# Six more weight units by in-place Prelu chains, other engines for three norms and four factors, and earlier joins in one window

## What is computed

```python
xn = layernorm(x)
K  = s4_kernel(...)                       # 512 taps from a 64-state model
conv = irfft(rfft(xn, 2L) * rfft(K, 2L))[:L] + D * xn
Wg, Wu, Wd = NF4_CODE[q] * absmax per block of 64   # 1792x512, 1792x512, 512x1792
h  = silu(xn @ Wg.T) * (xn @ Wu.T)
out = x + conv + h @ Wd.T
```

## Time and profile before

| | us |
|---|---|
| median of 3 runs | 469.33 (469.02 to 470.54) |
| the profiled execution, its own time | 468.54 |
| its span in the profile | 466.8 |
| PE busy | 436.9 (94%) |
| DVE busy | 400.3 (86%) |
| ACT busy | 279.8 (60%) |
| POOL busy | 205.0 (44%) |

### The profile page before, as it was taken

How to read it: one execution, slowest core, us unless ns; L and a number is a source line. 1 busy time by engine, 2 the same in 40 slices (tenths; PEclk the granted TensorE clock), 3 DMA queues, 4 the chain that set the end, 5 groups by cost and what they waited for, 6 DMA issues and landing times.

```text
span 466.8 us, 7247 instructions
## 1 busy us (share of the span) xinstructions
PE 436.9 (94%) x2544; PEld 248.0 (53%) x2544; DVE 400.3 (86%) x627; ACT 279.8 (60%) x475; POOL 205.0 (44%) x188
## 2 busy tenths in 40 slices
PE   0589999998994999999999999999999999999997
PEld 0444444443441444444444444466544688888886
DVE  5889958989987789898897778969898899999993
ACT  7956647477778686686775767946132543545340
POOL 0493586464958586456665555948400000000000
PEclk9999999999998999999999999999999999999999
DMA  8381636021514363151522142347693021101111
GB/s 283 79 289 69 136 76 157 24 68 46 181 34 148 116 197 137 46 181 46 180 68 68 37 115 78 92 162 241 197 345 136 1 91 46 38 10 46 46 47 45
DMA packets 34168, 51.41 MB, mean 110 GB/s; under 512 B 13076, under 2 KB 14164, under 8 KB 33364
## 3 DMA queue, kind: packets, MB, share of 16 engines
q1 hardware_dynamic: 34132, 50.95, 35.2%
HBM read 38.03 MB, written 10.81 MB: 105 GB/s over the span
## 4 chain that ended last, share of the span: by engine, by line
PE 64%; DVE 12%; POOL 11%; issue 5%; DMA 5%; ACT 3%; SPq 1%; POOLq 0%; DVEq 0%; ACTq 0%
PE bank L2278 27%; PE bank L2405 21%; PE bank L2355 8%; PE bank L2345 6%; DMA lines<-wd 3%; POOL work L879 2%; PE bank L2125 2%; DVE h L1421 1%; POOL w L892 1%; POOL h L784 1%; DMA work<-in_q_up 1%; DVE work L1351 1%; DVE h L1437 1%; DVE work L1347 1%; DVE h L1475 1%
## 5 line engine op out<-in xcount | busy, mean ns | idle before, releaser
L966 ACT ACTIVATE work<-work 128x512 f32<-128x512 f32 (+1 forms) x210 | 115.3, 622 | 13.1 <-POOL work L879 8.1
L879 POOL TENSOR_SCALAR work<-work 128x512 f32<-128x512 int32 x35 | 75.3, 2152 | 58.6 <-DVE work L1347 54.1
L2278 PE MATMUL bank<-h 128*128 128x512 f16 x360 | 81.7, 379 | 0.8 <-DVE h L1411 0.6
L2125 PE MATMUL bank<-xT,w 128*128 128x512 f16 (+1 forms) x300 | 64.5, 371 | 3.3 <-DVE w L1361 1.8
L2278 PEld LDWEIGHTS bank<-h 128*128 128x128 f16 x360 | 35.1, 98 | 44.3 <-issue 2.3
L2405 PE MATMUL bank<-wd,work 128*128 128x256 f16 x504 | 56.2, 273 | 0.0
L2278 PE MATMUL bank<-xT,w 128*128 128x512 f16 x240 | 55.4, 379 | 0.0
L2405 PEld LDWEIGHTS bank<-wd,work 128*128 128x128 f16 (+1 forms) x504 | 49.3, 98 | 6.0
L892 POOL TENSOR_SCALAR w<-work,sc 128x512 f16<-128x512 f32 x21 | 39.7, 1889 | 23.7 <-DVE work L1351 23.1
L2125 PEld LDWEIGHTS bank<-xT,w 128*128 128x128 f16 x300 | 29.1, 98 | 36.1 <-DVE w L1361 2.1
L1287 ACT ACTIVATE work<-h 128x896 f16<-128x896 f32 x30 | 27.9, 943 | 28.4 <-DVE h L2033 18.3
(11 more groups left out here) (198 smaller groups left out, 687.2 us busy)
## 6 DMA issues: line engine op xcount, KB each, us to landing
moved<-h SPq DMA_DIRECT2D x6, 1024.0 KB, 5.1
h<-moved SPq DMA_DIRECT2D x4, 1536.0 KB, 15.3
h<-in_x SPq DMA_DIRECT2D x8, 512.0 KB, 5.4
xT<-in_x SPq DMA_DIRECT2D x16, 256.0 KB, 3.7
out<-xT SPq DMA_DIRECT2D x15, 256.0 KB, 2.0
work<-in_q_gate SPq DMA_DIRECT2D x14, 256.0 KB, 2.9
work<-in_q_up SPq DMA_DIRECT2D x14, 256.0 KB, 3.4
work<-in_am_gate SPq DMA_DIRECT2D x28, 128.0 KB, 3.0
```

Source lines behind the costliest of these rows:

```text
L879: pool.tensor_scalar(chain_room(u, "r"), qs[:, u % 2, :], RIGHT_FROM, RIGHT_FROM, ALU.max, ALU.subtract).then_inc(first_done, 1)
L966: nc.scalar.activation(room, qs[:, u % 2, :] if j == 0 else room, KNEE, scale=scale, bias=bias, alpha=below).then_inc(knee_done, 1)
L2125: mm = nc.tensor.matmul(out_b, weights(k)[:, unit, wl, f, :], xT[:, TPC * c + first:TPC * c + last, xl, f, :], start=(i == 0), stop=(i == ...
L2278: mm = nc.tensor.matmul(out_b, weight(wl, f), token(xl, f), start=(n == 0 and i in (1, 5)), stop=(n == 5), skip_group_check=i not in (1, 5))
```

## The change

Five things.

1. Units 1 to 6 become chained too (`CHAINED` starts at 1). Their first pass is made by POOL, their six passes by ACT in the order l0, l1, l2, r0, r1, r2 (`SIDES_ORDER`), their high halves still by ACT. RIGHT and LEFT on DVE and `clamp` on ACT go away for them. The rooms of the sides and of the whole change with it, and with them what is waited for.
2. Norms of tiles 1 to 3 go from ACT to POOL; statistics of tile 4 go from ACT to DVE; the factors of chunk 1 go from POOL (17 operations) to DVE (12 operations).
3. The lists of the opening are written anew around this. On PE the 128 x 6 matmul that spreads the weight scales comes before `turn(1)`, and products of tile 1 are dealt between turns 4 to 7.
4. In window 5 the two joins of product 6 stand together right behind the first items; in mixed window 3 join (0, 3, 1) and `h_mul(15)` stand ahead of `token_whole(1, 3)` and an item.
5. On ACT `block_hi(3, 1)` comes before `copy_m1(0, 3)`, and the first two eighths of window 5's passes stand ahead of that window's `block_hi`.

```diff
+SIDES_ORDER = ("l0", "l1", "l2", "r0", "r1", "r2")
+def order_of(u):
+    return SIDES_ORDER if u < 7 else CHAIN_ORDER
-CHAINED = range(7, UNITS)
-POOL_HALVES = CHAINED
+CHAINED = range(1, UNITS)
+POOL_HALVES = range(7, UNITS)
...
         def chain_room(u, side):
-            return knee[:, u % 2 + (2 if side == "r" else 0), :]
+            right = side == "r"
+            if u in (3, 4):
+                return knee_1[:, 2 * (u - 3) + right, :]
+            return knee[:, (0 if u % 2 else 2) + right, :]
         def room_read(u):
-            return dq_after(u - 1, LEFT) if u == CHAINED[0] else dq_after(u - 2, WHOLE)
+            return None if u < 3 else dq_after(0, LEFT) if u < 5 else dq_after(u - 4 if u < 7 else u - 2, WHOLE)
...
-        SUMMED = (1, 4)
+        SUMMED = (1,)
+        POOL_NORMS = 1
...
@@ POOL's list @@
-            rstd(1)
+            first_pass(1)
+            for t in range(POOL_NORMS, TPC):
+                norm(t)
+            first_pass(2)
+            first_pass(3)
             for t in range(TPC, 2 * TPC):
                 norm(t)
+            first_pass(4)
+            first_pass(5)
             for i in range(14):
                 v_step(i)
+            first_pass(6)
...
@@ ACT's list @@
-            knees(1)
-            stats(4)
-            clamp(1)
-            for t in range(TPC):
-                norm(t)
+            chain(1, 0, 5)
+            norm(0)
+            chain(1, 5, 6)
+            chain(2, 0, 1)
...
-            make_knee(4, 2)
-            make_knee(4, 3)
+            chain(4, 0, 3)
             silu(0)
-            make_knee(4, 0)
-            make_knee(4, 1)
-            clamp(4)
-            make_knee(5, 2)
-            make_knee(5, 3)
+            chain(4, 3, 6)
+            chain(5, 0, 3)
             h_hi(0)
-            make_knee(5, 0)
-            make_knee(5, 1)
             silu(1)
             weight_hi(4)
-            clamp(5)
+            chain(5, 3, 6)
             h_hi(1)
...
             silu(12)
+            block_hi(BLOCKED[0], 1)
             copy_m1(0, BLOCKED[0])
-            block_hi(BLOCKED[0], 1)
...
@@ DVE's list, mixed window 3 @@
                     token_whole(1, 2)
+                    join(0, k, 1)
+                    h_mul(n + 3)
                     token_whole(1, 3)
+                    part(4, 6)
...
@@ DVE's list, window 5 @@
                     token_lo(1, 1)
                     stage_of(0, 2)
+                    join(0, k, 0)
+                    join(1, k, 0)
                     token_lo(1, 2)
-                    stage_of(2, 4)
-                    join(0, k, 0)
-                    stage_of(4, 5)
+                    stage_of(2, 5)
                     token_lo(1, 3)
                 stage_of(5, 6)
-                join(1, k, 0)
+                if both:
+                    join(1, k, 0)
...
@@ PE's list @@
             turn(0)
-            turn(1)
             pe.wait_ge(one_done, 1)
             pe.wait_ge(sc_done, 7)
             nc.tensor.matmul(bank[0][:, P:P + 6], ones[:], dg3, start=True, stop=True).then_inc(mx_bc, 1)
+            turn(1)
...
             turn(4)
+            products(1, (0,))
             turn(5)
-            products(1, (0,))
             turn(6)
+            pe.wait_ge(b_cp, 1)
+            pe.wait_ge(wlo_done, PLACE[3] + 1)
+            product(1, 1, 0, 2)
             turn(7)
-            pe.wait_ge(b_cp, 1)
-            products(1, (1,))
+            product(1, 1, 2, TPC).then_inc(up_done, 1)
```

More of the change, by code:

```diff
@@ L237, in ffn_conv_kernel @@
         knee, acc, qs, am, sil = rows_of(0, KNEES), rows_of(4, 3), rows_of(7, 2).bitcast(I32), rows_of(9, 2), rows_of(11, 2)
-        acc_l, acc_r, wt = (acc[:, i, :] for i in range(3))
         ident = sb("ident", [P, P], F32)
@@ L550, in ffn_conv_kernel @@
         OS_AT = {3: 1, 1: 2, 2: 3, 6: 4}
-        FIRST_STEPS = [(0, RIGHT), (0, LEFT), (1, RIGHT), (0, WHOLE), (0, SCALED), (1, LEFT), (1, WHOLE), (2, RIGHT),
-                       (1, SCALED), (2, LEFT), (3, RIGHT), (2, WHOLE), (3, LEFT), (2, SCALED), (3, WHOLE), (3, SCALED)]
         FIRST_BANK = (0, 4)
@@ L945, in make_knee @@
                     act.wait_ge(q_ld[u % 2], 16 * (u // 2 + 1))
-                reader = RIGHT if k >= 2 else LEFT
-                if u >= 2:
-                    act.wait_ge(dq_done, dq_after(u - 2 if u < 9 else u - 1, reader))
                 scale, bias, below = NF4_KNEES[k]
@@ L954, in chain_pass @@
             def chain_pass(u, j):
-                side, i = CHAIN_ORDER[j][0], int(CHAIN_ORDER[j][1])
+                order = order_of(u)
+                side, i = order[j][0], int(order[j][1])
                 room = chain_room(u, side)
                 if i:
-                    act.wait_ge(knee_done, PASSES_AT[u] + CHAIN_ORDER.index(f"{side}{i - 1}") + 1)
+                    act.wait_ge(knee_done, PASSES_AT[u] + order.index(f"{side}{i - 1}") + 1)
                 elif side == "r":
@@ L972, in knees, with chain @@
                     make_knee(u, k)
+            def chain(u, first, last):
+                for j in range(first, last):
+                    chain_pass(u, j)
             def clamp(u):
@@ L1174, in _ @@
             silu(2)
-            knees(6)
+            chain(6, 0, 6)
             silu(3)
-            clamp(6)
             silu(4)
@@ L1183, in _ @@
             x_hi(15)
-            for j in range(len(CHAIN_ORDER)):
-                chain_pass(7, j)
+            chain(7, 0, 6)
             silu(5)
@@ L1228, in mixed_window @@
                 part(k, 6, 8)
+                if k > 3:
+                    part(k + 1, 0, 2)
                 block_hi(k + 1, 0)
@@ L1249, in window @@
                     token_hi(1, 3)
-                    part(k, 0, 3)
+                    part(k, 2, 3)
                 part(k, 3, 6)
@@ L1605, in _ @@
             rstd(0, 5)
-            step(1, RIGHT)
+            step(0, WHOLE)
             rstd(0, 6)
@@ L1618, in _ @@
             scales(5)
+            stats(4)
+            scales(6)
+            step(0, SCALED)
             stats(5)
-            scales(6)
-            step(0, WHOLE)
             stats(6)
-            step(0, SCALED)
             scales(7)
@@ L1627, in _ @@
             moments(4, 8)
+            step(1, WHOLE)
+            rstd(1, 0)
+            rstd(1, 1)
+            rstd(1, 2)
             x_lo(0)
-            step(1, LEFT)
+            rstd(1, 3)
+            weight_lo(0)
+            rstd(1, 4)
             x_lo(1)
-            weight_lo(0)
-            step(1, WHOLE)
+            rstd(1, 5)
+            step(1, SCALED)
+            rstd(1, 6)
+            rstd(1, 7)
             x_lo(2)
-            step(2, RIGHT)
-            step(1, SCALED)
+            rstd(1, 8)
             x_lo(3)
+            rstd(1, 9)
+            rstd(1, 10)
             weight_lo(1)
-            step(2, LEFT)
-            step(3, RIGHT)
+            rstd(1, 11)
+            scales(9)
             step(2, WHOLE)
-            scales(9)
-            step(3, LEFT)
+            scales(10)
             step(2, SCALED)
-            scales(10)
+            scales(11)
+            weight_lo(2)
+            stats(8)
             step(3, WHOLE)
-            weight_lo(2)
+            scales(12)
             step(3, SCALED)
-            stats(8)
             x_lo(4)
-            scales(11)
+            x_lo(5)
             weight_lo(3)
-            x_lo(5)
-            scales(12)
             stats(9)
@@ L1667, in _ @@
             rstd(2, 3)
-            items(23, 24)
+            step(4, WHOLE)
             rstd(2, 4)
             rstd(2, 5)
-            items(24, 25)
+            step(4, SCALED)
             rstd(2, 6)
@@ L1678, in _ @@
             rstd(2, 11)
-            items(25, 26)
-            items(26, 27)
             weight_lo(4)
             h_lo(1)
-            items(28, 29)
+            step(5, WHOLE)
             x_lo(8)
-            items(29, 30)
+            step(5, SCALED)
             stats(12)
@@ L1696, in _ @@
             h_mul(3)
-            items(30, 31)
-            items(31, 32)
-            items(33, 35)
+            step(6, WHOLE)
+            step(6, SCALED)
             h_mul(4)
@@ L1755, in mixed_window @@
                     token_lo(1, 0)
-                part(4, 6)
-                join(0, k, 1)
-                h_mul(n + 3)
+                    part(4, 6)
+                    join(0, k, 1)
+                    h_mul(n + 3)
                 token_sum(1, 0 if k == 3 else 3)
@@ L2152, in turn @@
             def turn(t):
-                if t < TPC:
+                if t < POOL_NORMS:
                     pe.wait_ge(xn_done, t + 1)
                 else:
-                    pe.wait_ge(xp_done, t - TPC + 1)
+                    pe.wait_ge(xp_done, t - POOL_NORMS + 1)
+                if t >= TPC:
                     pe.wait_ge(xlo_done, t - TPC + 1)
```

60 lines of the change are left out of this document (26 added, 34 removed).

## The result

| | before | after |
|---|---|---|
| median of 13 runs each, us | 469.80 | 472.31 |
| lowest to highest | 467.88 to 471.90 | 469.58 to 475.07 |
| the profiled execution, its own time | 468.54 | 471.57 |
| its span | 466.8 | 469.7 |
| PE, DVE, ACT, POOL busy | 436.9, 400.3, 279.8, 205.0 | 440.0, 396.7, 280.8, 209.1 |

The ratio is 1.0051, 95% interval 1.0029 to 1.0074: the changed kernel is slower by about 2.4 us. I had forecast 468.8 us, no change, range 466.2 to 471.6. The sign is wrong and the time lies outside the range.

The account below looks back on a forecast made before the run. PE was taken to bound the kernel, busy 94% of the span, so only its idle gaps could give time. Opening +1.5 and middle -2.0 made -0.5 us on the median 469.33: 468.8 us, no change, range 466.2 to 471.6.

Parts of the forecast that it names:

- The walk of the opening: Engine lists walked with assumed durations up to the gathering of tiles 12 to 15: 53.2 instead of 52.68, +0.5 us.
- whatever moves 52.68 moves PE: DVE's gathering of the last four tiles' statistics at 52.68 moves DVE's stretch from 71.65, and PE waiting there.
- The toll of POOL: Ahead of SCALED of unit 1, POOL's new passes and norms lengthen DVE steps: about +1.0 us, bounds 0 and 2.0.
- The rival in which POOL blocks DVE for whole operations: DVE's steps from 8 to 20 us held for whole POOL operations: 475.3 us, half of it 472; chance 0.12.
- Opening: New opening lists, walk +0.5 plus POOL's toll +1.0: +1.5 us, bounds -0.8 and +3.1.
- (a): block_hi(3, 1) ahead of copy_m1(0, 3): DVE's 0.46 and PE's 0.55 waits go, 0.5 us sooner.
- (d): Four passes pulled ahead of block_hi(5) take some 2.1 us on ACT, which waits there anyway: 0.
- (b): Join (0, 3, 1) earlier: PE's 1.38 at 108.46 goes but is given back before join (0, 4, 0): 0.
- (c): Window 5 joins earlier: product 4 of tile 5 2.7 us sooner, six slow matmuls cost 1.2: -1.5 us.
- the joins give nothing: Rival: DVE late at SCALED before unit 13's high half, product 4 starts as now: 470.8 us, slower; chance 0.12.
- my signs of being right: No join wait before window 5's product 3, 4 to 5 us at product 4, passes 0.66 apart, gathering at 54.2.
- those of being wrong: Gathering of tiles 12 to 15 before 52.7 or after 56, or product 4 within 2 us of its products 7.

Follow-up runs that it names:

- warm run: Changed kernel with 12 extra matmuls of 256 columns between turn(3) and the first product; 471.85 us, ratio 1.0049.
- opening alone: Changed kernel with parts 4 and 5 of the change taken back; 472.36 against 469.66 us, ratio 1.0053.
- joins-only run: Kernel before with only the two joins of window 5 put together; 469.83 against 469.49 us, ratio 0.9993.

## Why the prediction was wrong

**The walk of the opening: +0.5 forecast.** The step that failed is "`h_hi(0)` starts at 39.5": it came at 41.88. The dependent pass was right (three of one side in 1.94, so (1.94 - 0.62)/2 = 0.66 from one to the next). From the split of tile 7 on, my walk held: it had 6.1 us to `h_hi(0)`, and 35.77 to 41.88 is 6.11.

What failed lies ahead of it: I had that split on ACT end near 33.4 and it ended at 35.87, with 4.8 us of standing for turns 5 and 7. Two causes can be told apart. The slow first products, which I did not expect at all: in the warm run, without them, `h_hi(0)` starts at 40.38, 1.5 sooner. And PE's own new list, part 3 of the change: turn 5 now stands behind the 12 matmuls at 27.97, and turn 7 behind the product at 33.33, which waits 1.74 for the low half of unit 3, which waits for ACT, which waits for turn 5. In the warm run, with its fast start, ACT still stands 1.62 and 2.33 for these two turns. No run put the turns back ahead of the products, so what their order costs, and whether that cures the opening as well as unit 4's passes do, stays open. Moving these passes into the waits brought `h_hi(0)` to 40.30 with the same slow products.

**What the opening moves.** I wrote that whatever moves 52.68 moves PE, and watched that row alone. My own walk had unit 5's low half end at 49.7, though PE before had reached that point at about 49 (12 matmuls of 2.75 into the 48 at 46.31) without a wait. So a second path, unit 5 straight to PE, was already late in my own numbers. That half ended at 51.56 + 0.75 = 52.31, and PE's 2.59 sets the end as much as the gathering does: the warm run freed one path and the other took over, for there PE came 1.5 sooner together with unit 5. The run that moved unit 4's passes brought unit 5 sooner and not PE.

**The toll of POOL: +1.0.** Right in kind, and no more than that. DVE, then POOL's norms (22.20) and a first pass (28.50):

```profile
19.00 0.68 DVE L1354 SCALAR_TENSOR_TENSOR work<-work 128x512 f32<-128x512 f32 x1
...
23.63 1.07 DVE L1354 SCALAR_TENSOR_TENSOR work<-work 128x512 f32<-128x512 f32 x1
...
28.65 1.00 DVE L1354 SCALAR_TENSOR_TENSOR work<-work 128x512 f32<-128x512 f32 x1
```

```profile
22.20 3.90 POOL L789 TENSOR_SCALAR h<-h 128x512 f32<-128x512 f32 x4 [3.90 <-DVE h L1584]
...
28.50 1.92 POOL L885 TENSOR_SCALAR work<-work 128x512 f32<-128x512 int32 x1
```

Steps of 0.68 take 1.07 under a norm and 1.00 under a first pass. But I had put the toll ahead of SCALED of unit 1, and that ended at 19.00 + 0.68 = 19.68, where my walk without the toll had 19.7: two small steps there took 0.53 and 0.58 instead of 0.17 (at 15.79 and 16.43, under first passes), and nothing of it shows at the end of SCALED. The rival in which POOL blocks DVE for whole operations, and with it the rule of the Trainium skill (SBUF — State Buffer, Who interferes with whom), would have held the step at 28.65 until the first pass of 28.50 ends at 30.42, 1.8 us; it was longer by 0.3. The measurement decides against the rule for first passes. For norms it doesn't: the norm over the step at 23.63 ends at 24.16, and a step of 0.68 from there would end at 24.84, where this one ends at 24.70. And POOL pays too: the norms at 11.44 and 13.52 take 0.77 each, the one at 12.20, into which DVE's SCALED of 12.38 falls, 1.33, while that DVE step keeps 0.67. So a norm and such a step seem to take turns, with now one and now the other waiting. In the stretch that the rival names, 8 to 20 us, only the two small steps were longer, 0.8 us together; that its half price, 472, is near the measured 472.3 is chance. No experiment took the first passes away from POOL, so the sum of the toll was not measured by itself.

**Opening: forecast +1.5, measured +2.5** (interval of the opening alone 1.6 to 3.4). A mis-sized term, inside its bounds of -0.8 and +3.1, and near the right size in part by luck: the walk, for which I had +0.5, is where the runs find the loss, and the toll of +1.0 doesn't show at its place.

**(a) `block_hi`: -0.5.** PE's 0.55 went and DVE's 0.46 too; not run alone. (d) the passes pulled ahead, forecast 0, were not run alone either.

**(b) Join (0, 3, 1): "given back, 0".** This step failed in its mechanism: it was +1.3, and I had given it no bound. I took join (0, 4, 0) as "isn't moved"; in the run with this edit alone it starts at 123.16, before at 121.74, since DVE itself was late. I asked when PE would need the join and not when `h_mul(15)`, which moved with it, would find its silu. ACT's silu was in the trace of before, started at 107.21 and ended at 107.90, 0.5 ahead of the old `h_mul` at 108.43: the old order had just enough room, and nothing in the profile's waits says so.

**(c) Window 5: -1.5.** The mechanism came as forecast: no wait for a join at product 3, a new one at product 4, slow matmuls behind it. Three sizes were off: the start 2.14 sooner and not 2.7, the wait 5.4 and not 4.6, and 12 slow matmuls for 1.9 us and not six for 1.2. Left: 0.25 to 0.3 by the joins alone. Join (0, 5, 1) in the joins-only run:

```profile
153.61 0.68 DVE L1449 TENSOR_TENSOR h<-bank,h 128x512 f32<-128x512 f32 x1
```

On before's scale (1.02 less) that is 152.59, 0.4 later than the 152.16 that I had kept, which takes 0.4 off the 2.7. Product 4 starts sooner not by its join, but because PE no longer stands behind the joins of product 6. The rival "the joins give nothing" had about the right size with the wrong cause. DVE does stand longer for POOL's half (1.88 in this run, before 1.33), but because DVE comes sooner: that half starts at 142.91, 141.89 on before's scale, where before it started at 141.83. The gain is small mostly by the slow clock behind the longer wait.

**Sum.** Opening +2.5, `h_mul(15)` +1.3, joins -0.3, `block_hi` up to -0.5: +3.0 against +2.5 measured, within what the intervals leave. My chance of slower, 0.24, rested on a toll of whole operations, which DVE did not pay in that stretch, and on joins without effect, which came near; the wait at unit 5 and the silu were in no rival. The price of the rival "the joins give nothing", +1.5 + 0, also left out the -0.5 of (a); it should have read 470.3. Of my signs of being right most came true (product 3 without a wait, 5.4 us at product 4, passes 0.66 apart, DVE idle ahead of `h_lo`, no wait at 95.27's row) and the gathering at 54.2 did not; of those of being wrong none did, 55.82 being just under 56. They watched the terms that I had, not the ones that I had left out.

## What to carry to other kernels

When an instruction is moved forward on an engine that runs its list in order, look up the end of every one of its inputs, and write down the slack of the old place: a wait that doesn't exist in the profile has no row. When a list is dealt anew, walk each engine's waits too, and put work that needs nothing into them; four passes moved ahead of two waits were worth 3.7 us. And a wait that is merged from two into one longer one can cost PE its clock: check what stands behind it, and fill it if nothing else can.
